# A graph layer's edge sums: thirteen column blocks for eight, and transposes of x that alternate between two PSUM banks

## The reference

```python
msg = node_feat[src] + edge_feat                       # one row of 128 for each edge
neigh = segment_sum(msg, dst, num_segments=3125)
rst = (1.0 + eps[0]) * node_feat + neigh
h = rst @ W1 + b1                                      # 128 -> 256
h = (h - mean(h, 0)) * rsqrt(var(h, 0) + 1e-5) * gamma + beta
out = relu(h) @ W2 + b2                                # 256 -> 128
return layernorm(node_feat + out)                      # over the features
```

## Time and profile before

| | us |
|---|---|
| median of 3 runs (lowest, highest) | 258.77 (257.5, 259.24) |
| the profiled execution | 256.72 |
| its span, first to last instruction | 254.9 |
| PE, busy in the span | 239.1 (94%) |
| DVE, POOL, ACT, busy in the span | 182.7, 178.7, 132.2 |

### The profile page before, as it was taken

The page is one execution under the profiler, slowest core; times in us unless marked ns, Lnnn a source line. Parts: engine busy times, 40 slices in busy tenths (PEclk is TensorE's granted clock), DMA queues, the critical chain, the costliest instruction groups (busy, mean ns, idle before and its releaser), DMA issues.

```text
span 254.9 us, 6747 instructions
## 1 busy us (share of the span) xinstructions
PE 239.1 (94%) x2147; PEld 197.8 (78%) x2150; DVE 182.7 (72%) x683; ACT 132.2 (52%) x235; POOL 178.7 (70%) x116
## 2 busy tenths in 40 slices
PE   7997799999999998999999999999999999999970
PEld 3775579989989977888878888888888889645960
DVE  5995757989888867888778687876667311378872
ACT  3365655646556553655554554444443330376793
POOL 4498888888888888888888888888888860550000
PEclk9999999999999999999999999999999999999995
DMA  3868987889988796898787788877756330000044
GB/s 67 236 172 188 230 194 169 186 166 216 208 207 180 193 206 154 194 192 206 180 172 183 191 174 184 180 163 169 169 119 156 74 39 3 0 0 3 3 126 130
DMA packets 51342, 38.13 MB, mean 150 GB/s; under 512 B 5099, under 2 KB 51099, under 8 KB 51305
## 3 DMA queue, kind: packets, MB, share of 16 engines
q1 hardware_dynamic: 36663, 30.89, 43.1%
q0 software_dynamic: 14400, 6.56, 21.5%
q10 hardware_dynamic: 242, 0.21, 0.3%
HBM read 36.05 MB, written 1.60 MB: 148 GB/s over the span
## 4 chain that ended last, share of the span: by engine, by line
PE 83%; DMA 6%; ACT 3%; DVE 3%; issue 2%; POOL 1%; ACTq 1%; another core or an unknown queue 0%; SPq 0%; DVEq 0%; POOLq 0%
PE ps L829 30%; PE ps L837 22%; PE ps L868 11%; PE ps L862 8%; PE ps L806 4%; DMA egat<-in_x_dram,srci 4%; PE ps L948 4%; PE ps L934 2%; PE ps L859 2%; DMA big<-in_src_dram 1%; ACT big L707 1%; DMA egat<-in_edge_attr_dram 1%; ACT big L665 1%; POOL egat L560 1%; ACT aggT L627 1%
## 5 line engine op out<-in xcount | busy, mean ns | idle before, releaser
L560 POOL DMA_INDIRECT egat<-in_x_dram,srci x100 | 168.8, 1688 | 36.4 <-issue 29.0
L665 ACT ACTIVATE big<-ps 128x500 f32 x158 | 96.4, 610 | 92.7 <-PE ps L868 62.7
L837 PEld LDWEIGHTS ps<-hit_c,ebuf 128*128 128x128 f32 x632 | 99.5, 188 | 9.6 <-DVE aggT L1214 2.9
L837 PE MATMUL ps<-hit_c,ebuf 128*128 128x20 f32 x632 | 94.6, 227 | 1.3 <-DVE aggT L1214 1.2
L1214 DVE TENSOR_TENSOR aggT<-aggT,ps 128x20 f32 x208 | 35.9, 173 | 51.1 <-PE ps L837 34.4
L829 PE MATMUL ps<-big,xN 128*128 128x120 f16 (+7 forms) x200 | 58.0, 292 | 1.1 <-ACT aggT L627 0.9
L829 PE MATMUL ps<-big,xr 128*128 128x120 f16 (+7 forms) x200 | 58.0, 292 | 0.0
L829 PE MATMUL ps<-big,x_room 128*128 128x120 f16 (+7 forms) x200 | 57.9, 292 | 0.0
L868 PE MATMUL ps<-hit_k,hit_l 128*128 128x375 f16 x158 | 53.6, 339 | 0.0
L862 PE MATMUL ps<-hit_k,hit_l 128*128 128x300 f16 x158 | 45.5, 288 | 0.0
L1128 DVE TENSOR_TENSOR hit_k<-iota_b,key 128x752 f16<-128x752 f16 x79 | 42.9, 543 | 0.0
(11 more groups left out here) (120 smaller groups left out, 206.5 us busy)
## 6 DMA issues: line engine op xcount, KB each, us to landing
ebuf<-in_edge_attr_dram SPq DMA_DIRECT2D x79, 256.0 KB
egat<-in_edge_attr_dram SPq DMA_DIRECT2D x49, 128.0 KB
egat<-in_x_dram,srci POOLq DMA_INDIRECT x100
xN<-in_x_dram SPq DMA_DIRECT2D x6, 256.0 KB, 4.3
out_dram<-big SPq DMA_DIRECT2D x5, 256.0 KB
w_sb<-in_L_gnn_W_dram SPq DMA_DIRECT2D x2, 128.0 KB
out_dram<-big SPq DMA_DIRECT2D x2, 128.0 KB
big<-in_src_dram ACTq DMA_DIRECT2D x1, 192.0 KB
```

The lines of the kernel that those rows point to most:

```text
L560: return nc.gpsimd.indirect_dma_start(to, None, x[:, :], bass.IndirectOffsetOnAxis(ap=ix, axis=0), compute_op=op)
L665: nc.scalar.activation(cnt[:, :, bass.ds(lows[m - load_from(m)], WIN)], ps[:, m % BANKS_C, 0:KEYS].rearrange("p (t n) -> p t n", n=WIN), A ...
L837: last = nc.tensor.matmul(ps[:, SUMS + w % BANKS_S, 0:WIN], rows_v[:, j * D:(j + 1) * D], hits_v, start=(j == 0), stop=(j == ROWS - 1))
```

## The change

There are thirteen blocks of 9 to 14 groups instead of eight of 10 to 31 (columns: 104, 152, 164, 182, 180, 196, 196, 210, 212, 210, 196, 196, 218, before 120, 180, 256, 376, 468, 466, 332, 218). The last block has 10 groups in both. Transposes of x alternate between banks 3 and 4 and wait for the copy of the piece before the last one; they stand in windows 0, 2, 3, 5, 7, 8, 10 instead of 0, 2, 4 ... 12, and four loads of x stand one window earlier. PE's three sums move from windows 3, 8, 15 to 9, 12, 15 and take piece 3 first; the first waits for six copies. DVE's splits move from 3, 6, 10, 14 to 5, 8, 12, 17. There are 14 fillers instead of 20. Two numbers of the planner change; the order of windows 0 to 18 stays. A wait between DVE's comparisons is put into the code for the groups below `PORT`, and `PORT` is 0, so it is in no group; its semaphore is counted up all the same.

```diff
-BLOCKS_C = (10, 12, 17, 25, 31, 31, 22, 10)
+BLOCKS_C = (9, 10, 11, 12, 12, 13, 13, 14, 14, 14, 13, 13, 10)
...
-SPLITS_W = (3, 6, 10, 14)
-RESTS_W = (3, 8, 15)
+SPLITS_W = (5, 8, 12, 17)
+RESTS_W = (9, 12, 15)
+TURNS_W = (0, 2, 3, 5, 7, 8, 10)
+PORT = 0
...
-HITS = 3200
+HITS = 3000
...
-GATHER_FIRST = 19000
+GATHER_FIRST = 18000
...
-FILLS = ((6, 2), (14, 1))
+FILLS = ((4, 2), (10, 1))
...
-        X_AT = [2 + X_LEAD * i for i in range(NB - 3)]
+        X_AT = [1 + X_LEAD * i for i in range(NB - 3)]
...
-        SUM_B = [early_g, early_g + 1, early_g - 1]
+        SUM_B = [early_g - 1, early_g, early_g + 1]
...
-        TURN_AT = [2 * i for i in range(NB)]
+        TURN_AT = list(TURNS_W)
+        BEFORE_SUMS = max(i for i in range(NB) if i % 2 == 1) + 1
...
                 if half == 0:
                     pe.wait_ge(x_loaded[b], 16)
-                    pe.wait_ge(key_made, 1)
-                    if i > 0:
-                        pe.wait_ge(x_scaled, i)
+                    if i == 0:
+                        pe.wait_ge(key_made, 1)
+                    if i == 1:
+                        pe.wait_ge(lo_made, 1)
+                    if i > 1:
+                        pe.wait_ge(x_scaled, i - 1)
...
-                    last = nc.tensor.transpose(ps[:, ACC, k:k + r], xN[0:r, t, :], ident[0:r, 0:r])
+                    last = nc.tensor.transpose(ps[:, ACC + i % 2, k:k + r], xN[0:r, t, :], ident[0:r, 0:r])
...
                 pe.wait_ge(x_loaded[b], 16)
                 if i == 0:
-                    pe.wait_ge(lo_made, 1)
                     pe.wait_ge(minus_made, 1)
+                    pe.wait_ge(x_scaled, BEFORE_SUMS)
...
-                                        keys[:, :, 0, :].unsqueeze(2).to_broadcast([P, 2, KEYS_A // 2, 2]), ALU.is_equal)
+                                        keys[:, :, 0, :].unsqueeze(2).to_broadcast([P, 2, KEYS_A // 2, 2]),
+                                        ALU.is_equal).then_inc(first_keys_made, 1)
+                if m < PORT:
+                    dve.wait_ge(first_keys_made, m // 2 + 1)
```

More of the change, by code:

```diff
@@ L315, in gnn_layer @@
         slot_hits_made = sem("slot_hits_made")
+        first_keys_made = sem("first_keys_made")
         key_hits_made = sem("key_hits_made")
@@ L426, in gnn_layer @@
         W_CLAMPS = READY[0] + 12
-        assert G_AT[0] > 3 and W_CLAMP < G_AT[0] + LAG and W_CLAMPS < min(C_AT[2 * LOADS], G_AT[CLAMP_G - GC])
+        assert G_AT[0] > 3 and W_CLAMP < G_AT[0] + LAG and W_CLAMPS < min(C_AT[2 * LOADS], (G_AT + [G])[CLAMP_G - GC])
         W_TESTS = READY[0] + 8
@@ L621, in _, with scale_x @@
                                  ps[:, 1, 0:GC].rearrange("p (h q) -> p q h", q=QC), ACT.Copy).then_inc(carry_made, 1)
-            def scale_x(i, turned, scaled, bank):
+            def scale_x(i, turned, scaled):
                 b = X_ORDER[i]
                 act.wait_ge(turned, i + 1)
-                nc.scalar.activation(aggT[:, b * BANK:b * BANK + width(b)], bank[:, 0:width(b)], ACT.Copy,
+                nc.scalar.activation(aggT[:, b * BANK:b * BANK + width(b)], ps[:, ACC + i % 2, 0:width(b)], ACT.Copy,
                                      scale=b2e[:, D:D + 1]).then_inc(scaled, 1)
@@ L657, in _ @@
                     if store_of(TURN_AT[i]) == m and C_AT[m] > TURN_AT[i]:
-                        scale_x(i, x_turned, x_scaled, ps[:, ACC, :])
+                        scale_x(i, x_turned, x_scaled)
                 act.wait_ge(counts_made, m + 1)
@@ L679, in _ @@
                 for i in range(NB):
-                    scale_x(i, gen_x_turned, gen_x_scaled, ps[:, ACC + i % 2, :])
+                    scale_x(i, gen_x_turned, gen_x_scaled)
                 store(gen_hidden_made, gen_hidden_stored)
```

## The result

| | before | after |
|---|---|---|
| median (lowest, highest), us | 259.0 (257.5, 261.78), 4 runs | 263.78 (263.13, 266.13), 4 runs |
| profiled execution, its span, us | 256.72, 254.9 | 264.42, 262.6 |
| mean granted clock of the profiled span | 0.989 | 0.964 |

The ratio is 1.0254 with a 95% interval of 1.0191 to 1.0316: slower, where I had forecast no change that can be told. Whether it is more than 2% the interval leaves open. The median lies just under the upper end of my range, where the rival of the falling clock stood. In this and the other ratios, runs over 1.5% above the fastest of their kernel are left out, while the medians are of all runs; those left out are mostly the ones with the lowest mean clocks, so the ratios understate what the clock costs.

The account below looks back on a forecast made before the run. PE's work bounds the kernel, plus what the first 31 us lose. 0.28 + 1.40 + 0.3 − 0.64 + 1.0 − 0.3 = +2.0 us on the median 258.77 gives 260.8 us; range 256.6 to 264.0.

Parts of the forecast that it names:

- the rival of the falling clock: Before window 6: PE's clock falls in 3.5 us of idle time, +1.2 to +3.6, taken as 263 us; chance 0.20.
- Window 6 kept its place: Window 6 still begins at 21.79, waiting for its gather; PE's idle time before it grows from 1.74 to about 3.5.
- PE's clock, kept at 1.00 in the sum: The sum has no clock cost; a fall in the idle stretch before window 6 is left to a rival.
- The rival with 0.20: The falling clock before window 6: half speed, +1.2 to +3.6 over the forecast, taken as 263 us; chance 0.20.
- +1.45: Up to window 13: window 12's two edge sums, +0.28, and one more sum, +1.17.
- 0.6: Window 13 to last block: `sum_last` +0.23, ACT-copy wait +0.3, fillers −0.64, block matmuls +1.0, DVE waits −0.3.
- The wait for piece 3: In window 9 the first sum waits some 2.8 us for x's last piece, issued at 23.1, landing 4.05 later.
- an edge sum priced at 0.14 us: Edge sums on PE taken at 0.14 each: window 12's two add +0.28, the loop's get no extra price.
- the 375 extra block matmuls: Thirteen blocks instead of eight: 375 more block matmuls at 2.7 ns each above their columns, +1.0 us.
- The waits of the middle: After 32 us smaller blocks give DVE more time, so part of PE's 0.56 wait goes: −0.3, bounds −0.56 to +1.0.
- Sums and fillers: One more sum from block 0 on, +1.40, its ACT-copy wait, +0.3, and four fillers gone, −0.64.
- The 2.05 us to the median: The profiled execution, 256.72, lay 2.05 below its runs' median, so the forecast adds this difference.

Follow-up runs that it names:

- e9_hold: Changed kernel with PORT = 10, counted windows' edge sums moved behind the counts' matmuls, and fillers where PE still waited: 256.43 us, ratio 0.9892.
- e1_fill: Changed kernel with 20 fillers in front of window 6: 262.2 us, ratio 1.0198.
- e6_all: Changed kernel with PORT = 10 and the edge sums of counted windows from 25 on behind the counts' matmuls: 257.1 us, ratio 0.9880.
- e4_edge: Changed kernel with the edge sums of counted windows from 25 on issued behind the counts' matmuls: 260.47 us, ratio 1.0138.
- the gap: In the first five pairs of groups DVE waits for its first comparison before starting the second; alone on the kernel before: 256.65 us, ratio 0.9886.
- e5_port: Changed kernel with PORT = 10 and nothing else: 261.58 us, ratio 1.0076.
- e10_before_gap: Kernel before with only the wait between DVE's comparisons, for the first five pairs of groups: 256.65 us, ratio 0.9886.

## Why the prediction was wrong, point by point

- **Window 6 kept its place: right.** 21.30 for 21.79, and the idle time grew to 3.29 us (3.5 forecast). That the second gather is the one that waits was wrong (it was the first), but the two together ended where I put them.
- **The step that failed first: PE's clock, kept at 1.00 in the sum.** The rival with 0.20 had the place, the mechanism and nearly the price. For window 13 the forecast was +1.45 (two edge sums and a sum), the trace has +5.30. The 3.85 us between them are what the low clock cost, less what it hid. From window 6 to window 13 PE's matmuls take 14.72 us without the waits; in e9_hold, where the clock held, the same ones take 9.0 (its 18 further fillers left out). Of these 5.7 us, 2.0 were hidden in the wait of window 9 (0.80 for 2.8) and up to 0.87 in the wait in front of block 0, which is gone, and the gather came 0.5 earlier. That leaves 2.3. The other 1.5 would be work that the sum did not have in front of window 13: 0.27 are six more matmuls of block 0, the rest stays open. I had put +1.2 to +3.6 on the clock. The Trainium skill (TensorE: Matmul & The Clock Gate, the section on HAM oscillation), which I had cited for 263, was borne out as to the fall of the clock. That the median, 263.78, comes so near to 263 is partly luck: 2.15 us of the span (+2.75 for 0.6) come from the blocks, which that rival did not have.
- **The wait for piece 3: hidden, not refuted.** SP issued the load at 23.57 (23.1 forecast). With PE at half speed the wait was 0.80 and named ACT. e1_fill and e6_all, where PE came earlier, show it: 1.77 and 1.88 us, for 2.8; the sum began 3.4 and 3.5 us behind SP's issue (at 23.10 and 21.40), where I had 4.05. On the way from there to block 0 I misread a row: from the start of ACT's copy to the start of the scale I took about 0.5 us, and the earlier trace rows have 1.00 (29.57 to 30.57). The sum would have been +2.5 with it, which decides nothing.
- **The second step that failed: an edge sum priced at 0.14 us, the step of the earlier trace rows, wherever it stood.** The sum had a price for the 375 extra block matmuls, and it was right: what successive block matmuls occupy above columns / 2.4 rose from 1.44 to 2.50 us in the middle stretch, 2.9 ns for each of 368 more (2.7 forecast). What I left out is the instruction behind them. The rows behind 120 columns in the trace of before already had 0.20. 4.11 us of edge sums stand in the loop for which the sum had none.
- **The waits of the middle: right in sign, too small.** Block matmuls and waits fell by 0.97 us in spite of these added 1.06; 0.25 are columns of block 0 that moved in front of window 13, so 1.8 us in front of the blocks' followers went, not 0.3. I had counted the 0.56 of the earlier trace rows as the one longer wait after 38 us. The trace of before has a second, also gone after the change:

```profile
96.28 0.40 PE L837 MATMUL ps<-hit_c,ebuf 128*128 128x20 f32 x2 [0.68 <-DVE aggT L1214]
```

- **Sums and fillers: nearly right.** −0.63 for −0.64; +0.22 where 0.3 of wait and 0.23 of `sum_last` stood.
- **The 2.05 us to the median.** I took them as a constant. They were not: the profiled execution of before never lost its clock before the end (0.989). Of the runs of before beside e1_fill, the one with a mean clock of 0.991 took 255.14 us, four at 0.985 took 256.87 to 259.38. So the kernel before, too, seems to pay for the clock in many of its runs, and a forecast from the rows of one of its better runs left that out on both sides. The clock is not all of it: one run at 0.976 took 257.50.

Together: +1.45 and 0.6 forecast for the two stretches, +5.30 and +2.75 measured, −0.35 behind the loop, +7.70 in all for +2.0. For the first cause e1_fill gives back 2.37 of the 3.85 us, and the clock falls again at the next wait; for the second e4_edge takes 3.16 of the 4.11 us off the edge sums, and its whole loop is 3.98 shorter.

## What to carry to other kernels

When an edit makes one kind of matmul narrower, price the instruction that follows it as well: f32 weights need a wide matmul in front (here 256 columns or more left only the 26 to 29 ns), and the existing trace has such pairs at several widths. When an edit takes work away ahead of a wait that it does not shorten, the idle time grows, and what PE's clock does there belongs into the sum, for the median and not for the one profiled run. Cut the traces at the same points of the program before naming a cause: here the two causes stood in different stretches and one number hid both.

## What the runs showed of the hardware

- One gather was held up by 4 us or more in every kernel without the gap (5.71, 5.78, 6.04, 7.91 us for the slower of the first two), and never with it: the longest of the first two was 2.32. DVE ended 11 instructions in between before and 12 after the change, so it is not the end of one instruction that lets POOL in; a wait for a semaphore in DVE's row of comparisons does. The Trainium skill (SBUF — State Buffer, the box on the "DVE blocks DMA" trap) describes POOL shut out during one instruction; these runs show it for a row of them. Whether any pause would do was not tried. In all seven kernels without the gap the long gather ends 1.54 to 1.65 us, about its usual length, after DVE starts to add an edge sum, as the earlier trace rows show it for the one before; but other additions passed without letting it in (one at 14.21 in the same trace), so what decides stays open.
- The clock does not need one long pause to fall. In e5_port it fell at 24.7, in the third of three waits of 0.58, 0.76 and 0.92 us from 19.5 on; in e10_before_gap at 30.8, after 0.85, 0.27 and 0.87 us between 25.3 and 30.2, while the kernel before kept it through 0.85 and 0.87 in the same places. Runs of one kernel differ with it, though not by it alone: of e5_port, 258.15 us at a mean clock of 0.992 and 261.27 at 0.970, but 261.25 at 0.982.
- A first f32 matmul of 20 columns behind a block matmul of 104 to 468 columns occupies PE for 137 ns less the time of that matmul, and at least 26, within 4 ns (medians). Behind the 375 columns of `counts_b` in e4_edge it is 33.
